# A decoder layer on one core: attention and expert stages in one block, the expert weights' pieces made in attention's last steps

## The reference

```python
# 1. a decaying complex running sum over the 32 sequences, times x
x = layernorm(x + conv(x).real * x)
# 2. cross attention: 16 heads of 16 channels, relu on q, k and v
Qp, Kp, Vp = relu(x @ Wq + bq), relu(ctx @ Wk + bk), relu(ctx @ Wv + bv)
out = softmax(q @ k.T / 4) @ v + Qp
x = layernorm(x + (ln_g * normalized(out) + ln_b))
# 3. experts: each token goes to the nearest of 8 centroids
xn = rms_norm(x, scale)
ids = argmin(dist2(xn, centroids))
a, g = split(xn @ up_w[ids])             # 256 -> 2 x 512
x = layernorm(x + (a * silu(g)) @ down_w[ids] + x)   # 512 -> 256
```

## Time and profile before

| | us |
|---|---|
| median of 3 runs | 1278.97 |
| lowest and highest | 1272.46, 1282.16 |
| the profiled execution | 1285.39 |
| its span, first to last instruction | 1283.3 |
| PE busy in the span | 1114.9 (87%) |
| DVE busy | 953.8 (74%) |
| ACT busy | 664.2 (52%) |
| POOL busy | 792.0 (62%) |

### The profile page before, as it was taken

One profiled execution on the slowest core, in us unless ns is written; L12 is line 12 of the kernel. 1 busy time (PEld: TensorE's weight loads), 2 busy tenths in 40 slices (PEclk: granted clock), 3 DMA queues, 4 the chain that ended last, 5 costly groups with the idle time before them and its releaser, 6 DMA issues. The chain is left out here.

```text
span 1283.3 us, 27523 instructions
## 1 busy us (share of the span) xinstructions
PE 1114.9 (87%) x8060; PEld 817.8 (64%) x8061; DVE 953.8 (74%) x2411; ACT 664.2 (52%) x1413; POOL 792.0 (62%) x943
## 2 busy tenths in 40 slices
PE   0599999999999998999999999830999999999996
PEld 0465666666666666666666666520788888888885
DVE  6357799899899899899899898639455555555553
ACT  1247577676677677776776677514322222222221
POOL 6545778888788888888887865344133333333333
PEclk9859899999899999999999999755999999999998
DMA  5556755655556646656556555206011111111110
GB/s 143 131 158 173 189 144 143 154 138 150 141 142 149 160 130 153 151 146 155 142 146 152 141 134 128 76 25 180 25 53 49 44 52 49 52 46 47 53 49 22
DMA packets 90827, 144.92 MB, mean 113 GB/s; under 512 B 12663, under 2 KB 78336, under 8 KB 84513
## 3 DMA queue, kind: packets, MB, share of 16 engines
q1 hardware_dynamic: 84192, 126.61, 38.3%
q0 software_dynamic: 6528, 16.99, 4.5%
HBM read 91.44 MB, written 53.03 MB: 113 GB/s over the span
## 5 line engine op out<-in xcount | busy, mean ns | idle before, releaser
L888 DVE TENSOR_REDUCE neg_max_sb<-S 128x2 f32<-128x512 f32 x512 | 327.9, 682 | 78.6 <-PE S L693 77.6
L559 ACT ACTIVATE probs<-T 128x512 f32<-128x512 f32 x512 | 278.5, 595 | 152.4 <-PE T L706 140.5
L693 PE MATMUL S<-k_st,q_st 48*128 48x256 f32 x1024 | 215.4, 320 | 51.5 <-DMA k_st<-k_pieces 26.0
L693 PEld LDWEIGHTS S<-k_st,q_st 48*128 48x128 f32 x1024 | 146.7, 193 | 131.1 <-issue 56.3
L706 PE MATMUL T<-q_st,k_st 49*128 49x256 f32 x1024 | 210.5, 318 | 3.7 <-ACT probs L559 2.1
L706 PEld LDWEIGHTS T<-q_st,k_st 49*128 49x128 f32 x1024 | 145.6, 192 | 21.0 <-ACT probs L559 16.2
L1201 ACT ACTIVATE gT<-GT 128x512 f32<-128x512 f32 x71 | 42.6, 600 | 207.5 <-PE GT L1236 207.5
L669 PE MATMUL O<-probs,v_aug 128*32 128x256 f32 x2048 | 147.1, 408 | 0.7 <-ACT probs L559 0.7
L1177 POOL DMA_INDIRECT out<-res,token x71 | 76.4, 1076 | 101.5 <-DVE res L1309 101.5
L1258 PE MATMUL Y<-dn_sb,gT 128*128 x568 | 134.2, 379 | 0.8 <-ACT gT L1201 0.8
L513 POOL DMA_INDIRECT buckets<-row,slot x64 | 66.2, 1034 | 90.4 <-DVE slot L1052 80.2
(11 more groups left out here) (177 smaller groups left out, 2551.6 us busy)
## 6 DMA issues: line engine op xcount, KB each, us to landing
q_st<-q_pieces SPq DMA_DIRECT2D x64, 256.0 KB, 4.7
k_st<-k_pieces SPq DMA_DIRECT2D x64, 256.0 KB, 5.9
xr<-buckets SPq DMA_DIRECT2D x71, 129.0 KB, 2.1
xt<-in_x SPq DMA_DIRECT2D x32, 256.0 KB, 6.4
ct<-in_ctx SPq DMA_DIRECT2D x32, 256.0 KB, 6.8
up_sb<-in_L_ffn_up_w SPq DMA_DIRECT2D x8, 1024.0 KB, 8.6
q_pieces<-q_hi SPq DMA_DIRECT2D x32, 256.0 KB, 2.1
q_pieces<-q_lo SPq DMA_DIRECT2D x32, 256.0 KB, 2.1
```

The lines of the kernel that those rows point to most:

```text
L559: a_.activation(probs[:, h % 8].rearrange("p k t -> p (k t)"), T_ps[h % 2][:, :], ACT.Exp, scale=DH ** -0.5).then_inc(s["exp_ok"], 1)
L693: last = t_.matmul(S_ps[h % 2][:, c * TOK:(c + 1) * TOK], q_st[base:base + STACK, h, c * P:(c + 1) * P], k_st[base:base + STACK, h, :], st ...
L888: v.tensor_reduce(neg_max[:, cur.mod(2), :, h], S_ps[h % 2][:, :].rearrange("p (c t) -> p c t", c=NTC), AX.X, ALU.max, negate=True).then_i ...
```

## The change

- There is one block. Each engine's expert part is called at the end of its attention part (`sync2(sp)`, `gpsimd2(pool)`, `scalar2(act)`, `tensor2(pe)`, `vector2(dve)`), with no barrier. In place of the barrier stand semaphore waits: on SP for the last scatters, on ACT ahead of the first high piece, and on PE as before.
- Tiles of the two stages still share memory, in another order: `up_hi` lies on buffers of the q, k and context work that are free by step 31, its last three experts on `v_aug` and `probs`; `dn_sb` lies on `q_st` and `k_st`.
- ACT makes high piece e at the step and head given in `HI_AT`, DVE low piece e as in `LO_AT`; POOL makes none. DVE does all eight where it did five.
- Up weights are uploaded in steps -2 to 5, where the last two were in steps 31 and 32.
- SP loads the down weights after the last transposed score. The tails are written half by SP and half by ACT.
- POOL makes the two tables of numbers, and zeros for the running sum, in the set-up.
- The running sum is three adds of eight numbers, each shifted by 1, 2 and 4; the table has 18 operations where it had 23.
- ACT runs a silu of one number ahead of the first tile, which loads the table of that function.

```diff
-UP_STEPS = (-2, -1, 0, 1, 2, 3, SEQ - 1, SEQ)
+UP_STEPS = (-2, -1, 0, 1, 2, 3, 4, 5)
+HI_AT = {(SEQ - 1, 3): (0,), (SEQ - 1, 7): (1,), (SEQ - 1, 13): (2,), (SEQ, 3): (3,), (SEQ, 5): (4,), (SEQ + 1, 5): (5, 6, 7)}
+LO_AT = {(SEQ, 0): (0, 1), (SEQ, 4): (2,), (SEQ, 9): (3,), (SEQ, 13): (4,), (SEQ + 1, 15): (5,), (SEQ + 2, 1): (6, 7)}
+HI_EARLY = 5
...
+            def tails(eng, part):
+                eng.wait_ge(z["table"], 2)
+                for e in range(part * E // 2, (part + 1) * E // 2):
+                    r = eng.value_load(tail_row[0:1, e:e + 1], min_val=0, max_val=PAD - P)
+                    eng.dma_start(buckets[bass.ds(r, P), :], pad_row[:, :]).then_inc(z["tails"], 16)
...
+            def sync(sp):
+                sp.wait_ge(s["t_pe"], H * SEQ)
                 for e in range(E):
                     dst = dn_sb[:, e * DNW:(e + 1) * DNW].rearrange("p (o n) -> p o n", o=HCH)
                     sp.dma_start(dst, down_w[e].rearrange("(o p) n -> p o n", p=P)).then_inc(z["down_in"], 16)
-                sp.wait_ge(z["table"], 2)
-                for e in range(E):
-                    r = sp.value_load(tail_row[0:1, e:e + 1], min_val=0, max_val=PAD - P)
-                    sp.dma_start(buckets[bass.ds(r, P), :], pad_row[:, :]).then_inc(z["tails"], 16)
+                tails(sp, 0)
+                sp.wait_ge(s["pads"], 16)
+                for p in range(2):
+                    sp.wait_ge(scat[p], 16 * NTC * SEQ // 2)
                 sp.wait_ge(z["tails"], 16 * E)
                 sp.wait_ge(z["table"], TABLE)
...
+            def scalar(act):
+                a_.activation(gate[0:1, 0:1], neg_half[0:1, :], ACT.Silu)
+                tails(act, 1)
...
-                setup(v.tensor_copy(ends[:, 0:1], tiles[:, 0:1]))
-                for e in range(1, E):
-                    setup(v.tensor_tensor(ends[:, e:e + 1], ends[:, e - 1:e], tiles[:, e:e + 1], ALU.add))
+                for k, w in enumerate((1, 2, 4)):
+                    a, b = scan[:, k % 2], scan[:, 1 - k % 2]
+                    setup(v.tensor_tensor(b[:, E:2 * E], a[:, E:2 * E], a[:, E - w:2 * E - w], ALU.add))
...
+                def upper(e):
+                    if e == 0:
+                        act.wait_ge(s["ups"], 16 * E)
+                        act.wait_ge(s["qn_pe"], SEQ)
+                        act.wait_ge(s["q_cut"], SEQ)
+                        act.wait_ge(s["k_cut"], SEQ)
+                        act.wait_ge(s["x1_ok"], 2 * SEQ)
+                        for half in range(2):
+                            act.wait_ge(stack_in[half], 64 * SEQ)
+                    if e == HI_EARLY:
+                        act.wait_ge(s["pv"], 4 * SEQ)
+                    at = slice(e * UPW, (e + 1) * UPW)
+                    a_.activation(up_hi[:, at], up_sb[:, at].bitcast(F32), ACT.Copy).then_inc(z["up_hi"], 1)
...
+                        for e in HI_AT.get((t.k, h), ()):
+                            upper(e)
...
+                        for e in LO_AT.get((t.k, h), ()):
+                            lower(e)
...
+                def lower(e):
+                    dve.wait_ge(z["up_hi"], e + 1)
+                    at = slice(e * UPW, (e + 1) * UPW)
+                    v.tensor_tensor(up_sb[:, at], up_sb[:, at].bitcast(F32), up_hi[:, at].bitcast(F32), ALU.subtract).then_inc(z["lo_dve"], 1)
```

More of the change, by code:

```diff
@@ new lines, in build @@
+        o = sb1("o", [P, NTC, C])
+        oq = sb1("oq", [P, NTC, C])
+        y1, y2 = o, oq
+        xnT = sb1("xnT", [P, NCH, TOK])
+        xw = sb1("xw", [P, NTC, C])
+        junk = sb1("junk", [P, C], BF16)
+        bq_sb = sb1("bq_sb", [P, NCH])
+        bk_sb = sb1("bk_sb", [P, NCH])
+        bv_cut = sb1("bv_cut", [P, NTC * C], BF16)
+        scale_col = sb1("scale_col", [P, NCH])
+        g_bc = sb1("g_bc", [P, C])
+        b_bc = sb1("b_bc", [P, C])
+        decay = sb1("decay", [P, 2, C])
@@ new lines, in build @@
+        decay_im2, decay_re = decay[:, 0], decay[:, 1]
+        centT = sb1("centT", [P, NCH, E])
+        cent_sq = sb1("cent_sq", [P, NCH, E])
+        cent_norm = sb1("cent_norm", [P, E])
+        ones_r = sb1("ones_r", [P, P], F32R)
+        ones_bf = sb1("ones_bf", [P, P], BF16)
+        before = sb1("before", [P, P], BF16)
+        expert_no = sb1("expert_no", [P, NTC, E])
+        st1 = sb1("st1", [P, NTC, 6])
+        mv1 = sb1("mv1", [P, NTC, 2])
+        rs1 = sb1("rs1", [P, 2, NTC])
@@ new lines, in build, with wait, wait_value @@
+        s = {n: sem(n) for n in names.split()}
+        x_in, ctx_in_s, q_out, k_out, stack_in = ([s[a + "0"], s[a + "1"]] for a in ("x_in", "ctx_in", "q_out", "k_out", "stack"))
+        neg_in, scat = [s["neg_in0"], s["neg_in1"]], [s["scat0"], s["scat1"]]
+        def wait(eng, name, item, per=1, j=None):
+            if not item.runtime and item.k >= SEQ:
+                item, j = Item(0, SEQ - 1), per
+            wait_value(eng, name, item.times(per, per if j is None else j))
+        def wait_value(eng, name, v):
+            sm = s[name] if isinstance(name, str) else name
+            if isinstance(v, int):
+                if v > 0:
+                    eng.wait_ge(sm, v)
+            else:
+                eng.wait_ge(sm, v)
+                after_register_wait(eng)
@@ new lines, in wait_ring, with after_register_wait, steps @@
+        def wait_ring(eng, sm, item, ring, per):
+            if not item.runtime:
+                while item.k >= SEQ:
+                    item = item - ring
+            wait_value(eng, sm, item.uses(ring) * per)
+        def after_register_wait(eng):
+            if eng.engine in (mybir.EngineType.Pool, mybir.EngineType.SP):
+                eng.sem_inc(s["pool_waits" if eng.engine == mybir.EngineType.Pool else "sp_waits"], 1)
+        def steps(eng, body):
+            for n in range(-2, SEQ + 3):
+                body(Item(0, n))
@@ L237, in steps @@
             def steps(eng, body):
-                for n in range(-2, SEQ + 3):
+                lead = 4
+                loops = (NTILES - 2 - lead) // UNROLL
+                for n in range(-2, lead):
+                    body(Item(0, n))
+                with eng.Fori(0, loops) as i:
+                    for k in range(UNROLL):
+                        body(Item(i, lead + k))
+                for n in range(lead + UNROLL * loops, NTILES + 2):
                     body(Item(0, n))
             def active(item):
-                return item.within(0, SEQ)
@@ new lines, in scalar, with step @@
+            def scalar(act):
+                a_ = nc.scalar
+                a_.activation(gate[0:1, 0:1], neg_half[0:1, :], ACT.Silu)
+                tails(act, 1)
+                def step(t):
+                    m, n = t - 1, t + 1
+                    if active(m):
+                        wait(act, "gT_pe", m)
+                        wait(act, "y_pe", m - 2)
+                        a_.activation(gT[:, m.mod(2)], GT_ps[:, :], ACT.Copy).then_inc(z["gT_ok"], 1)
+                    if active(t):
+                        wait(act, "g_pe", t)
+                        wait(act, "gated_ok", m)
+                        a_.activation(gate[:, :], G_ps[:, :], ACT.Silu).then_inc(z["gate_ok"], 1)
+                    if active(n):
+                        wait(act, "xsT_pe", n)
+                        wait(act, "a_pe", n - 2)
+                        a_.activation(xsT[:, n.mod(2), 0], XT_ps[:, 0:NCH * P], ACT.Copy).then_inc(z["xsT_hi"], 1)
+                steps(act, step)
@@ L253, in _ @@
+            return sync, gpsimd, scalar, tensor, vector
+        sync2, gpsimd2, scalar2, tensor2, vector2 = experts()
+        with nc.Block() as block:
             @block.sync
```

602 lines of the change are left out of this document (256 added, 346 removed).

## The result

The changed kernel took 1271.2 us in the median of 20 runs (1258.8 to 1285.7); the kernel before, run beside it on the same chip, took 1283.1 in the median of 20. The ratio is 0.990, 95% interval 0.988 to 0.993, which is 12.8 us faster (9.6 to 15.9), where 16.4 was forecast. (The ratio leaves out the executions that fell into a second, slower state, three of the changed kernel's twenty among them; so it gives 12.8 where the two medians differ by 11.9.) Two later comparisons of the same pair gave 0.993 (0.990 to 0.997) and 0.988 (0.983 to 0.994). The profiled execution took 1271.59 us, span 1269.8; that of before had 1283.3.

The account below looks back on a forecast made before the run. PE bounds the expert stage, PE and DVE steady attention; between them PE idles 39.8 us. 30.5 - 3.8 - 1.9 - 5.4 - 3.0 = 16.4 us gained, 1262.6 us at the median, chance 0.45; range 1248 to 1275.

Parts of the forecast that it names:

- rival B: Attention's end stretches more: tails 5.8 us, port lock and uploads at their ceilings; gain 7.6, 1271.4 us; chance 0.22 with D.
- slow tails: Before the first tile read: tails keep landing in 5.8 us instead of 2.7, cutting the gross gain to 27.4 us.
- dearer lock: At attention's end: the DVE-POOL port lock costs its ceiling of 9.4 us, 4 more than the 5.4 taken.
- Gross gain, 30.5: Between attention and experts: PE's first transpose of `xs` comes at 867.9 instead of 898.42, 30.5 us earlier.
- rival D: Something else holds the first tile, say SP waiting for tails or scatter: a few us kept back; chance within B's 0.22.
- signs that the prediction named for being wrong: Attention's end longer by 20 us or none, first tile read waiting after the table, or steady steps or experts changing pace.
- ACT, 3.8: Eight high pieces of 1.81 us in attention's last steps cost 3.8 us; floor nothing, ceiling 14.5.
- DVE and the lock, 1.9 + 5.4 = 7.3: Attention's end: eight 2.22 us low pieces cost DVE 1.9 us, and waits between POOL and DVE 5.4.
- Uploads, 3.0: Two 1 MB uploads moved from steps 31 and 32 to steps 4 and 5 lengthen those, 3.0 us; possibly nothing to 4.7.
- signs named: Hole 10 to 12 us, adds under 0.3, attention's end 11 longer, steps 4 and 5 2 longer, experts 385.
- Rival A: Attention's end: idle time hides most pieces and uploads cost nothing; about 4 us lost, 26.5 saved, 1252.5 us; chance 0.28.
- rival C: Steps 31 to 34: all pieces lie in the chain, 32.3 us plus 4.7 for uploads; 6.5 slower, 1285.5 us; chance 0.05.

Follow-up runs that it names:

- no low pieces: The changed kernel without DVE's eight low pieces, the products reading whole weights instead: 1256.39 us in one run, the kernel before 1283.05.
- sum alone: The kernel before with only the running sum made in three shifted adds: 1287.01 us in one run, the kernel before 1287.92.
- two late kernels: The changed kernel with low pieces behind the tile table; high pieces also later (1270.4 us, ratio 0.989) or left in place (1281.65 us, one run).
- sum with all low pieces on DVE: The kernel before with three shifted adds and all eight low pieces on DVE, none on POOL: 1281.94 us in one run, before 1287.92.

## Why the prediction was right in direction and high by 4 us

The forecast was 16.4 us, and 12.8 (9.6 to 15.9) were measured. In absolute times 1262.6 us was forecast and 1271.2 came, which is rival B's 1271.4; but the kernel before took 1283.1 in the same comparison where the forecast started from 1278.97, so the differences are what can be compared, and 12.8 lies between the forecast's 16.4 and B's 7.6. B asked for three things at once: the slow tails came, the dearer lock in part, the cost of the uploads not at all. So the size is partly luck: terms failed in opposite directions. By the three profiled executions, the cut gives 485.5 us before and 476.9, 472.6 and 472.6 after: 8.6 to 12.9 us. Its terms:

- **Gross gain, 30.5.** 26.5, 26.5 and 27.8 us. The step that failed is that the tails take the scatter's 2.7 us because the down weights are gone: they took 3.9 and 4.8, beside a scatter of 4.9 (3.4, 3.7 and 4.1 in the third execution). Another 0.8 us is their later start, 1.2 us behind the cast instead of 0.4. The branch with slow tails, 27.4, was the right one. That the table takes 6.0 us, that nothing of the barrier is left, and that SP would stand on tails or scatter (rival D, as a mechanism, 5.4 us behind the table) were right; SP's wait had been left out of the sum. It is also one of the signs that the prediction named for being wrong: the first tile's read waits for something after the table.
- **ACT, 3.8.** Between 1.8 (no low pieces, 65.4, against sum alone, 63.6) and 4.3 us (the two late kernels). Against the sum with all low pieces on DVE, 62.2, where the clock falls at nearly the same place, it is 3.2 us: 2.6 in step 31 to 32, where 2.5 was forecast, and 0.6 behind it. Right in size.
- **DVE and the lock, 1.9 + 5.4 = 7.3.** 7.4 to 10.8. The step that failed is "the first four are in step 32, where DVE waits for PE most of the time: free", with 0.8 for the lock: the first three together held POOL's root for 7.05 us and with it `xw`, `junk` and the exponentials. With the fifth piece, 1.8 us were forecast up to the id copy of step 33, and 4.1, 1.3 and 4.1 measured. For the sixth it was 1.8 against 2.3 to 2.6, and for the last two 3.2 against 3.4 to 4.1: these were nearly right. At the last two the lock took 4.1 us of the root in the first execution and 1.9 in the others, for the 2.4 taken.

The Trainium skill (SBUF — State Buffer, section "SBUF: two separate sides") says that the one that starts second is blocked for the other's whole instruction. The trace goes further, with 7.05 us through three instructions of 2.2, and in another execution 2.65 us for the same root.

- **Uploads, 3.0.** Nothing, by a comparison of their own. The step that failed is reading two long steps in the earlier trace rows as the price of what was issued in them: the same steps are 24.7 and 24.4 us in another execution of the kernel before. In the changed kernel the two steps with the moved uploads are 24.0 and 23.5 us long, against a mean of 23.9; the sign of 2 us more did not come.
- **Not in the sum:** the clock. It fell 11 to 13 us earlier in all three executions of the changed kernel; two unchanged attention stages in which it did were 2.0 to 3.7 us longer. And the expert stage is 0.7 to 1.8 us longer; the two kernels with only the sum changed, whose expert stage is that of before, take 387.0 us for it too, so this needn't be the change's doing.

Sum by the first execution: 26.5 - 16.3 - 1.6 = 8.6, with the missing 4.9 of the two spans' difference of 13.5 before step 31, where executions differ anyway. By the second execution it is 26.5 - 12.9 - 0.7 = 12.9. The uploads' 3.0 that weren't lost mostly paid for the tails; what is left over is attention's end, 12.9 to 16.3 us where pieces, lock and all were to cost 11.1, and the expert stage. Of the signs named: the hole was to be 10 to 12 us (14.1, 12.8 once), the adds under 0.3 each (0.18), attention's end 11 us longer than 57.8 from the same exponentials (they start at 797.24 now, behind the first high piece: 71.8, 14.0 longer), the expert stage 385 (386), steps 4 and 5 2 us longer (they were not). Rival A (pieces hidden) is out by no low pieces against after; rival C was nowhere near, since the high pieces cost an eighth to a third of their 14.5 us and the low ones about half of their 17.8.

## What to carry to other kernels

Work moved "into an idle engine" must be priced by what the *other* engines do at that moment: here DVE's idle time in step 32 was POOL's busy time, and the pieces shut POOL out: five pieces cost 4.1 us that way, and 1.3 where POOL got its turns. Put behind POOL's work, two cost 0.3 us in step 32, but one cost its full 2.2 us in step 33, so look at each place by itself and not at the total. Look first for idle time behind the last dependency of the next stage: DVE waited 7.6 us for the first tile, long enough for three and a half pieces, and moving all low pieces there was as fast, within the intervals, as the careful interleaving. A long step with an event in it is no price of the event; change the event alone, or read a second execution, before it enters a sum.

## What was not expected of the hardware

- Back-to-back DVE operations with two SBUF inputs can hold a POOL operation off through all of them (0.71 us became 7.05, in two executions of three) or let it in behind each (2.65, 2.71, 3.31). The same program does either. The difference was worth 2.8 us in step 32, with the clock the same. A POOL indirect DMA's issue, too, went from 0.98 to 2.97 us beside such a piece.
- A short table operation can inherit the wait that a rewrite took from another: the running sum fell from 14.17 us to 0.53, and three operations behind them rose to 3.7, 4.2 and 4.4.
- TensorE's granted clock falls to 1.2 GHz near the end of attention some 18 or some 6 us behind the same instruction, in kernels with the same attention code, at a price of 2.0 to 3.7 us.
- Eight small writes of 129 KB and a scatter issued together took 3.4 to 5.0 us to land (medians of three executions), where the scatter alone took 2.7.
